# A transposed accumulator: the accumulator of a streaming cross-attention is kept in blocks of 32x32, VectorE transposes in place of TensorE, and the probabilities are transposed one head at a time

## The chip, the cores and the metric

The kernel runs on one core of a Trainium2 chip. The metric is the device time of one execution in microseconds.

## The reference

A set of 512 queries (M, 512x512) attends over 6250 inputs x (6250x256) with 8 heads of 64; then follow an output projection, a layer norm, a feed-forward block of width 2048 and a second layer norm. Everything is float32.

```python
q = (M @ Wq.T).reshape(e, h, dh).transpose(1, 0, 2)
kv = x @ Wkv.T + bkv
k, v = jnp.split(kv, 2, axis=-1)
...
sim = jnp.einsum('hid,hjd->hij', q, k) * dh ** (-0.5)
sim = jnp.where(mask, sim, -1000000000.0)
attn = jax.nn.softmax(sim, axis=-1)
out = jnp.einsum('hij,hjd->hid', attn, v)
out = out.transpose(1, 0, 2).reshape(e, h * dh)
out = out @ Wo.T + bo
m = layer_norm(out + M)
ffn = jax.nn.relu(m @ W1.T + b1) @ W2.T + b2
z = layer_norm(ffn + m)
```

## The kernel before

**Tiling.** The keys are padded to 7 chunks of 896. The 8 heads are 4 pairs; two heads of 64 fill the 128 partitions. The 512 queries are 4 tiles of 128. A chunk holds 4 pairs, and a pair 4 tiles, so there are 28 pairs and 112 tiles. Products other than the one with V are made from a high and a low part of each operand (three matmuls in place of one).

**One tile (S, E, X).** TensorE writes the scores of a query tile, both heads, into two of three PSUM slots of 1024 columns (line 889). VectorE adds the mask (`lower`), takes the running minimum of the negated scores and writes them to `prob` (line 734, one instruction for each head). ScalarE takes the exponential in place and sums the rows (line 579, one for each head). VectorE then transposes both heads' 1792 columns in blocks of 32x32 from `prob` into `st` (line 744, step X). In the order of the steps X of a tile stands behind the two minima of the next tile, and the first of these minima waits for the X before it (`prob` has two buffers).

**The moves (M, B).** Blocks of 32x32 are transposed in place, so the quarters of partitions have to change places: 16 DMAs for each half pair (two tiles) carry `st` into `pt`, twelve issued by SyncE (M, line 387), four by ScalarE (B, line 631). X of the first tile of a half waits until the moves of the pair before have landed.

**The values (W, C, F, A).** Two pairs later TensorE multiplies `val` with `pt` over 7 key tiles (W, line 943; fp32, four passes each), which gives outT with head dimensions on partitions and 512 queries in columns. ScalarE copies it to SBUF (C, line 610), TensorE transposes it with four matmuls against the identity (F, line 952), and VectorE adds it to the accumulator `acc`, queries on partitions (A, line 751).

**The rest of a pair.** K makes the next pair's keys (line 815), ScalarE copies them (H, line 602) and GpSimd splits them (L). V makes a value tile of the next chunk, copied by ScalarE (line 588). Z updates the statistics: GpSimd takes the difference of maxima (`drop`), ScalarE its exponential (`alpha`, line 635), and GpSimd scales the row sums and `acc` (line 472), one factor for each query and head. J and R load and split x, Q loads the mask.

**The end.** After the last pair N divides `acc` by the row sums (line 757), G transposes it on TensorE (line 963), T and D add the bias and split it (lines 614 and 760), and Y projects with Wo (line 847), for pairs 0 and 1, then 2, then 3. The two last pairs' W, C, F and A lie between these.

**What sets the order.** It is written out by hand. `ROUNDS` (line 52) has a string for each tile of each pair, `FIRST` (line 74) those of the first two pairs, and `chunk_schedule` (line 86) turns them into one list of steps, with a list of its own for the end. Each engine walks the same list and takes its own steps in that order, so a step's place in the list is its place in each queue. Semaphores tie the engines together.

```python
for c in range(CHUNKS):
    body(c, chunk_schedule(c == 0, c == CHUNKS - 1), c % 2)
```

## Time and profile before

| | |
|---|---|
| median of three runs | 683.79 us (680.31, 683.79, 1226.24) |
| the profiled execution | 684.72 us, span 682.9 us |
| TensorE matmul | 632.4 us busy (93%), 3382 instructions |
| VectorE | 549.7 us busy (80%), 685 instructions |
| ScalarE | 363.8 us busy (53%), 659 instructions |
| GpSimd | 254.8 us busy (37%), 312 instructions |
| attention (first scores to last exponential) | 20 to 541 us |
| output projection, norms, feed-forward | from there to the end |
| granted TensorE clock | 0.98 of full speed, mean |

The page gives one profiled execution. The span is the time from its first to its last instruction. Engines work side by side, so their busy times do not add up to it. A matmul's end is modelled, and a matmul overlaps the next, so TensorE is read better by the starts of its instructions. A line of a timeline has the start, the duration, the engine, the line of the program, what is written from what, and in brackets how long the engine had been idle before and who released it. DMA issues are shown on the queue of the engine that issues them (SPq, ACTq).

### The profile page before, as it was taken

The page shows a single profiled execution, that of the slowest core. Times are in us where ns is not written, and L with a number is a line of the kernel's source. Part 1 is how long each engine was busy: PE and PEld are TensorE (multiplying, and loading weights), DVE is VectorE, ACT ScalarE, POOL GpSimd, SP SyncE. Part 2 cuts the span into 40 slices and gives each one's busy share as a digit, 9 for nine tenths or more (in the row PEclk, how much of TensorE's full clock was granted, in tenths as well). Part 3 has the DMA queues.
Part 4 walks back from the last instruction along what each step waited for, and adds up shares of the span by engine and source line. Part 5 has one row for each costly group of instructions (what it writes and reads, how often), then busy time and mean ns, then how long its engine had stood idle before and what let it go on. Part 6 is the DMA issues. An engine that isn't in the chain of part 4 may idle for free.

```text
span 682.9 us, 10600 instructions
## 1 busy us (share of the span) xinstructions
PE 632.4 (93%) x3382; PEld 396.0 (58%) x3382; DVE 549.7 (80%) x685; ACT 363.8 (53%) x659; POOL 254.8 (37%) x312
## 2 busy tenths in 40 slices
PE   4999999999999999999999999999998697999996
PEld 3675555545665555655555566555653344688884
DVE  3889999999998999899999999899998836334334
ACT  5576565565565566556565565556564313333332
POOL 3561632264224632163226522363212404422224
PEclk9999999999999999999999999999999898799999
DMA  8078989878988889888997888888777982032221
GB/s 285 9 201 210 221 215 254 206 201 211 230 222 206 216 215 252 192 206 209 233 230 196 212 223 227 204 218 207 198 194 187 257 231 72 31 93 93 92 91 61
DMA packets 56098, 128.29 MB, mean 188 GB/s; under 512 B 15856, under 2 KB 20976, under 8 KB 55792
## 3 DMA queue, kind: packets, MB, share of 16 engines
q1 hardware_dynamic: 45296, 101.97, 58.2%
q10 hardware_dynamic: 10752, 25.70, 14.1%
q8 instruction: 25, 0.41, 0.3%
q14 instruction: 25, 0.20, 0.1%
HBM read 23.80 MB, written 1.05 MB: 36 GB/s over the span
## 4 chain that ended last, share of the span: by engine, by line
PE 59%; DVE 16%; issue 7%; SPq 5%; ACT 4%; POOL 3%; DMA 3%; ACTq 2%; DVEq 0%; POOLq 0%
PE tail L943 16%; PE slot L889 13%; DVE st L744 7%; PE tail L815 7%; PE slot L1001 7%; PE slot L996 7%; PE slot L815 6%; SPq L387 4%; DVE prob L734 4%; ACT prob L579 2%; PE tail L952 2%; ACTq L631 2%; DVE acc L751 2%; DMA wq_raw<-in_wq 1%; PE slot L847 1%
## 5 line engine op out<-in xcount | busy, mean ns | idle before, releaser
L579 ACT ACTIVATE prob<-prob,negmax 128x896 f32<-128x896 f32 x224 | 233.6, 1043 | 203.9 <-DVE negmax L734 201.4
L734 DVE CUSTOM_DVE_ANT_0 prob<-slot,lower,negmax_old 128x896 f32<-128x896 f32 x224 | 248.9, 1149 | 36.1 <-PE slot L889 25.4
L744 DVE STREAM_TRANSPOSE st<-prob 128x1792 f32<-128x1792 f32 x112 | 228.5, 2040 | 4.9 <-DMA pt<-st 4.7
L943 PE MATMUL tail<-pt,val 128*64 128x512 f32 x784 | 184.5, 607 | 8.1 <-ACT outT_sb L610 5.9
L943 PEld LDWEIGHTS tail<-pt,val 128*64 128x64 f32 x784 | 51.4, 138 | 102.9 <-issue 94.4
L889 PE MATMUL slot<-k_hi,q_hi 64*128 64x448 f32 x448 | 94.8, 414 | 10.9 <-DVE negmax L734 6.8
L889 PEld LDWEIGHTS slot<-k_hi,q_hi 64*128 64x128 f32 x448 | 43.3, 183 | 78.7 <-issue 71.2
L889 PE MATMUL slot<-k_hi,q_lo 64*128 64x448 f32 x448 | 84.0, 363 | 0.0
L889 PE MATMUL slot<-k_lo,q_hi 64*128 64x448 f32 x448 | 83.7, 362 | 0.0
L467 POOL TENSOR_TENSOR total<-total,alpha 128x8 f32<-128x8 f32 x28 | 5.8, 206 | 189.6 <-ACT alpha L635 189.5
L489 POOL TENSOR_TENSOR k_lo<-k_raw,k_hi 128x896 fp32r<-128x896 f32 x27 | 57.1, 2115 | 3.9 <-POOL k_hi L486 0.2
L442 POOL TENSOR_SCALAR lower<-mask_raw 128x896 bf16<-128x896 uint8 x28 | 27.1, 968 | 52.8 <-DVE negmax L734 41.8
L889 PEld LDWEIGHTS slot<-k_hi,q_lo 64*128 64x128 f32 x448 | 43.8, 184 | 2.6
L889 PEld LDWEIGHTS slot<-k_lo,q_hi 64*128 64x128 f32 x448 | 43.8, 185 | 1.1
L524 POOL TENSOR_TENSOR hid_lo<-hid,hid_hi 128x512 fp32r<-128x512 f32 x15 | 20.6, 1371 | 62.2 <-DVE hid_hi L799 62.2
L815 PE MATMUL tail<-wv_hi,x_hi 128*128 128x512 f32 x98 | 35.7, 445 | 6.9 <-ACT val L588 6.8
L579 ACT ACTIVATION_READ_ACCUMULATOR prob<-prob,negmax 128x1 f32 x224 | 41.7, 186 | 0.0
L815 PE MATMUL slot<-x_hi,wk_hi 128*128 128x448 f32 x112 | 33.5, 381 | 8.3 <-ACT x_hi L554 8.3
L799 DVE CAST hid_hi<-hid 128x512 fp32r<-128x512 f32 x15 | 6.4, 428 | 33.9 <-ACT hid L670 33.8
L815 PE MATMUL slot<-x_lo,wk_hi 128*128 128x448 f32 x112 | 32.6, 373 | 0.0
L815 PE MATMUL slot<-x_hi,wk_lo 128*128 128x448 f32 x112 | 32.3, 370 | 0.0
L670 ACT ACTIVATE hid<-slot,b_sb 128x512 f32<-128x512 f32 x16 | 11.0, 690 | 36.8 <-PE slot L996 36.8
(127 smaller groups left out, 844.6 us busy)
## 6 DMA issues: line engine op xcount, KB each, us to landing
pt<-st SPq DMA_DIRECT2D x672, 112.0 KB, 3.0
pt<-st ACTq DMA_DIRECT2D x224, 112.0 KB, 3.4
w_raw<-in_w SPq DMA_DIRECT2D x32, 256.0 KB, 2.9
x_raw<-in_x SPq DMA_DIRECT2D x13, 448.0 KB, 4.3
mask_raw<-in_mask SPq DMA_DIRECT2D x7, 448.0 KB, 4.5
mt_raw<-in_mt SPq DMA_DIRECT2D x2, 512.0 KB, 7.8
wo_raw<-in_wo SPq DMA_DIRECT2D x1, 1024.0 KB, 6.9
m_res<-in_mn SPq DMA_DIRECT2D x1, 1024.0 KB, 5.1
```

The costliest lines, as they stand in the source:

```text
L387: sp.dma_start(pt[LANES * b:LANES * b + LANES, buf, a], st[LANES * a:LANES * a + LANES, i, b]).then_inc(landed[buf], 16)
L442: nc.gpsimd.tensor_scalar(lower[:, t], mask_raw[:, t], -1.0, -BIG, ALU.add, ALU.mult).then_inc(lower_ready, 1)
L489: nc.gpsimd.tensor_tensor(kst[1][:, p % 2], k_raw[:], kst[0][:, p % 2], ALU.subtract).then_inc(klo_done, 1)
L524: nc.gpsimd.tensor_tensor(hid_split(i + j, j, 1), hid[:, j], hid_split(i + j, j, 0), ALU.subtract).then_inc(hidlo, 1)
L579: nc.scalar.activation(unit, unit, ACT.Exp, bias=negmax[:, p, u:u + 1], scale=-1.0, accum_out=psumrow[:, p, u:u + 1]).then_inc(exp_done, 1)
L734: nc.vector.tensor_tensor_reduce(out=prob[:, i % 2, h].rearrange("p (b n) -> p b n", b=2), in0=slot[:, j, :, :HALF], in1=lower[:, i].rearr ...
L744: nc.vector.transpose(st[:, g].rearrange("p b k (t i) -> p k b t i", t=2)[:, :, :, t2], prob[:, i % 2].rearrange("p h (k b i) -> p (h k) b ...
L815: last = nc.tensor.matmul(dst, stationary(a, k), moving(b, k), start=(n == 0), stop=(n == len(terms) - 1))
L889: last = nc.tensor.matmul(slot[:, j, b, :HALF], q2[qa][rows(h), p, P * i:P * i + P], key_half(p, b, kb)[rows(h)], start=(part == 0), stop= ...
L943: last = nc.tensor.matmul(outT[DH * h:DH * h + DH], val[:, val_at(i, parity ^ (p < 0)), head(p, h)], moving, start=(i == 0), stop=(i == KT ...
L996: last = nc.tensor.matmul(slot[:, 2, j], w12[a][:, j, k], mT2[b][:, k], start=(i == 0), stop=(i == len(terms) - 1))
L1001: last = nc.tensor.matmul(slot[:, t // 2, t % 2], hid_split(n, j, a)[:, P * t:P * t + P], w2_split(n, j, b), start=first and i == 0, stop= ...
```

## The change

The accumulator is kept as VectorE's block transpose leaves it: partition 32 d + i holds query i of a block of 32 and block d of the 128 head dimensions; the columns are 16 query blocks of 32 dimensions.

- C is a VectorE transpose of outT from PSUM into SBUF, in the place of ScalarE's copy; it moves from the third tile of a pair to the fourth, between the minima and X. F, the four TensorE transposes, is gone.
- A, the add, is done by GpSimd in all pairs but the last two of the last chunk, from SBUF.
- The factor `alpha` is needed for each query block and head in the new layout: 16 small ScalarE exponentials of 32 partitions by 4 columns (step e, eight in the third and eight in the fourth tile) write it from `drop` into `alpha_blk`. The scaling of `acc` by GpSimd becomes a step of its own (z) in the first tile of the next pair, three tiles later than before.
- X is two transposes of 896 columns, one for each head, each with its own count of `xposed`; each minimum waits only for its own head's half.
- At the end the reciprocal of the row sums is spread with 16 copies a pair (step i), G is a VectorE transpose into `prob`, and T and D read it from there. Y of pairs 0 and 1 stands wholly between the value products of the last two pairs, where it used to start before them.

```diff
-    ('S E0 E1 W0 W1 W2 W3 X M1 R0',
+    ('S E0 E1 W0 W1 W2 W3 X M1 R0 z',
      'S E0 V1 E1 Z K H L X B1',
-     'S E0 E1 F W4 W5 W6 C A X M0 Q',
-     'S E0 E1 V2 X B0'),
-    ('S E0 E1 W0 W1 W2 W3 X M1',
+     'S E0 E1 W4 W5 W6 X e0 M0 Q',
+     'S E0 E1 V2 C A X e1 B0'),
+    ('S E0 E1 W0 W1 W2 W3 X M1 z',
      'S E0 V3 E1 Z K H L X B1',
-     'S E0 E1 F W4 W5 W6 C A X M0',
-     'S E0 E1 V4 X B0'),
-    ('S E0 V5 E1 W0 W1 X M1',
+     'S E0 E1 W4 W5 W6 X e0 M0',
+     'S E0 E1 V4 C A X e1 B0'),
+    ('S E0 V5 E1 W0 W1 X M1 z',
      'S E0 V6 E1 Z K H J0 L X B1',
-     'S E0 E1 F W2 W3 W4 A X R1 M0',
-     'S E0 E1 W5 W6 C X B0 J1 I'),
-    ('S E0 E1 W0 W1 W2 W3 X M1',
-     'S E0 E1 Z F K H L A X B1',
-     'S E0 E1 W4 W5 W6 C X M0',
-     'S E0 E1 N0 X B0 O'),
+     'S E0 E1 W2 W3 W4 X e0 R1 M0',
+     'S E0 E1 W5 W6 C A X e1 B0 J1 I'),
+    ('S E0 E1 W0 W1 W2 W3 X M1 z',
+     'S E0 E1 Z K H L X B1',
+     'S E0 E1 W4 W5 W6 X e0 M0',
+     'S E0 E1 N0 C A X e1 B0 O'),
...
-                elif kind in "WC":
+                elif kind in "WCA":
                     step = (kind, p - 2, i)
-                elif kind in "FA":
-                    step = (kind, p - 3, i)
                 elif kind in "KHL":
                     step = (kind, p + 1, i)
                 elif kind in "MB":
                     step = (kind, p - i, i)
-                elif kind == "Z":
+                elif kind in "Ze":
                     step = (kind, p - 1, i)
+                elif kind == "z":
+                    step = (kind, p - 2, i)
                 if first and step[1] < 0 or last and (kind in "JRQ" or step[1] == PAIRS) or not last and kind in "IO":
                     continue
                 out.append(step)
-                if kind == "A" and last and step[1] >= 0:
-                    out.append(("N", step[1], 0))
     if last:
         a, b = PAIRS - 2, PAIRS - 1
-        out.extend([("F", 1, 0), ("A", 1, 0), ("N", 1, 0)])
-        out.extend([("X", b, 3), ("M", b, 1), ("B", b, 1), ("Z", b, 0), ("I", b, 1), ("O", b, 1)])
-        out.extend([("G", 0, 0), ("T", 0, 0), ("D", 0, 0)])
-        out.extend([*(("W", a, kt) for kt in range(3)), ("G", 1, 0), ("T", 1, 0), ("D", 1, 0)])
-        out.extend([*(("W", a, kt) for kt in range(3, KT)), ("C", a, 0), ("Y", 0, 0), ("F", a, 0), ("A", a, 0), ("N", a, 0)])
-        out.extend([("Y", 0, 1), ("Y", 0, 2), ("Y", 0, 3), ("G", a, 0), ("T", a, 0), ("D", a, 0)])
-        out.extend([*(("W", b, kt) for kt in range(KT)), ("C", b, 0), ("Y", 1, 0), ("F", b, 0), ("A", b, 0), ("N", b, 0)])
-        out.extend([("Y", 1, 1), ("Y", 1, 2), ("Y", 1, 3), ("G", b, 0), ("T", b, 0), ("D", b, 0)])
-        out.extend([("Y", 2, t) for t in range(QT)])
+        out.extend([("X", b, 3), ("M", b, 1), ("B", b, 1), ("Z", b, 0), ("e", b, 0), ("e", b, 1), ("z", a, 0), ("z", b, 0)])
+        out.extend([("I", b, 1), ("O", b, 1), ("i", 0, 0), ("N", 0, 0), ("G", 0, 0), ("i", 1, 0), ("N", 1, 0), ("G", 1, 0)])
+        out.extend([("T", 0, 0), ("D", 0, 0), ("T", 1, 0), ("D", 1, 0), ("i", a, 0)])
+        out.extend([*(("W", a, kt) for kt in range(KT)), ("C", a, 0), ("A", a, 0), ("N", a, 0), ("G", a, 0), ("T", a, 0), ("D", a, 0)])
+        out.extend([*(("Y", 0, t) for t in range(QT)), ("i", b, 0)])
+        out.extend([*(("W", b, kt) for kt in range(KT)), ("C", b, 0), ("A", b, 0), ("N", b, 0), ("G", b, 0), ("T", b, 0), ("D", b, 0)])
+        out.extend([*(("Y", 1, t) for t in range(QT)), *(("Y", 2, t) for t in range(QT))])
...
+        def per_block(stat, p):
+            return stat[:, p].unsqueeze(2).to_broadcast([P, BLOCKS, LANES])
+
+        def quadrants(*heads):
+
+            for dims in (d for h in heads for d in (2 * h, 2 * h + 1)):
+                for queries in range(QUAD):
+                    yield dims, queries, dims // 2
+
+        def block_stat(stat, p, dims, queries):
+
+            own = stat[LANES * dims:LANES * dims + LANES, p]
+            return own.rearrange("p (g q t) -> p q g t", g=2, q=QUAD)[:, queries]
+
+        def tile_stat(stat, p, queries, h):
+            own = stat[LANES * queries:LANES * queries + LANES, p, QT * h:QT * h + QT]
+            return own.rearrange("p (g t) -> p g t", g=2)
+
+        def by_block(t):
+            return t.rearrange("p (b i) -> p b i", b=BLOCKS)
+
+        def ao_raw(p):
+            return prob[:, p // 2, p % 2, :E]
...
+                    if kind == "z":
+                        n, own = pair_no(c, p), p % PAIRS
+                        blocks = in_register(pool, QUAD * QUAD * (n + 1))
                         if is_past(n, PAIRS):
                             pool.wait_ge(acc_added, n - PAIRS + 1)
-                        nc.gpsimd.tensor_tensor(by_head(acc[:, own]), by_head(acc[:, own]), per_head(alpha, own), ALU.mult).then_inc(acc_scaled, 1)
+                        pool.wait_ge(zeroed, 2)
+                        pool.wait_ge(alpha_blk_ready, blocks)
+                        nc.gpsimd.tensor_tensor(acc[:, own], acc[:, own], per_block(alpha_blk, own), ALU.mult).then_inc(acc_scaled, 1)
...
+                    if kind == "A" and not (final and p >= PAIRS - 2):
+                        posed, own = in_register(pool, pair_no(c, p) + 1), acc[:, p % PAIRS]
+                        pool.wait_ge(zeroed, 2)
+                        pool.wait_ge(acc_scaled, posed)
+                        pool.wait_ge(outT_copied, posed)
+                        nc.gpsimd.tensor_tensor(own, own, by_block(outT_sb[:]), ALU.add).then_inc(acc_added, 1)
...
-                    if kind == "C":
-                        act.wait_ge(pv_done, KT * (n + 1))
-                        if isinstance(n, int) and n == 0:
-                            act.wait_ge(qlo_done, PAIRS)
-                        if is_past(n, 1):
-                            act.wait_ge(f_filled, n)
-                        nc.scalar.copy(outT_sb[:].rearrange("p (g t a i) -> p g a t i", g=2, a=QUAD, t=2),
-                                       outT.rearrange("p (g a t i) -> p g a t i", g=2, a=QUAD, t=2)).then_inc(outT_copied, 1)
                     if kind == "T":
-                        act.wait_ge(aoT_filled, p + 1)
-                        nc.scalar.activation(ao2[0][:, p], gather_bank(p), ACT.Identity, bias=bv_sb[:, p:p + 1]).then_inc(aohi, 1)
+                        act.wait_ge(ao_ready, p + 1)
+                        nc.scalar.activation(ao2[0][:, p], ao_raw(p), ACT.Identity, bias=bv_sb[:, p:p + 1]).then_inc(aohi, 1)
...
+                    if kind == "e":
+                        if is_past(n, PAIRS):
+                            act.wait_ge(acc_scaled, n - PAIRS + 1)
+                        for dims, queries, h in quadrants(i):
+                            nc.scalar.activation(block_stat(alpha_blk, p % PAIRS, dims, queries), tile_stat(drop, p % PAIRS, queries, h),
+                                                 ACT.Exp).then_inc(alpha_blk_ready, 1)
...
-                        free = in_register(dve, QT * n + i - 1) if is_past(QT * n + i, 2) else None
                         for h in range(2):
                             j, before = unit_use(c, p, i, h)
                             written, u = in_register(dve, before + 1), QT * h + i
+                            free = in_register(dve, 2 * (QT * n + i - 2) + h + 1) if is_past(QT * n + i, 2) else None
                             dve.wait_ge(zeroed, 2)
-                            if h == 0 and free is not None:
+                            if free is not None:
...
-                        dve.wait_ge(exp_done, U * n + 2 * i + 2)
-                        nc.vector.transpose(
-                            st[:, g].rearrange("p b k (t i) -> p k b t i", t=2)[:, :, :, t2],
-                            prob[:, i % 2].rearrange("p h (k b i) -> p (h k) b i", b=QUAD, i=LANES)).then_inc(xposed, 1)
-                    if kind == "A":
+                        for h in range(2):
+                            dve.wait_ge(exp_done, U * n + 2 * i + h + 1)
+                            nc.vector.transpose(
+                                st[:, g].rearrange("p b (h k) (t i) -> p h k b t i", h=2, t=2)[:, h, :, :, t2],
+                                prob[:, i % 2, h].rearrange("p (k b i) -> p k b i", b=QUAD, i=LANES)).then_inc(xposed, 1)
+                    if kind == "C":
+                        read, done = in_register(dve, n) if is_past(n, 1) else None, in_register(dve, KT * (n + 1))
+                        dve.wait_ge(zeroed, 2)
+                        if read is not None:
+                            dve.wait_ge(acc_added, read)
+                        if isinstance(n, int) and n == 0:
+                            dve.wait_ge(qlo_done, PAIRS)
+                        dve.wait_ge(pv_done, done)
+                        nc.vector.transpose(by_block(outT_sb[:]), by_block(outT)).then_inc(outT_copied, 1)
+                    if kind == "A" and final and p >= PAIRS - 2:
                         dve.wait_ge(acc_scaled, n + 1)
-                        dve.wait_ge(f_filled, n + 1)
-                        own = acc[:, p % PAIRS].rearrange("p t n -> p (t n)")
-                        nc.vector.tensor_tensor(own, own, tp, ALU.add).then_inc(acc_added, 1)
-                    if kind == "N":
+                        dve.wait_ge(outT_copied, n + 1)
+                        nc.vector.tensor_tensor(acc[:, p], acc[:, p], by_block(outT_sb[:]), ALU.add).then_inc(acc_added, 1)
+                    if kind == "i":
                         dve.wait_ge(stats_kept, 2 * (n + 1))
                         nc.vector.reciprocal(inv[:, p], total[:, p]).then_inc(inv_ready, 1)
+                        dve.wait_ge(inv_ready, p + 1)
+                        dve.wait_ge(acc_scaled, n + 1)
+                        for dims, queries, h in quadrants(0, 1):
+                            nc.vector.tensor_copy(block_stat(alpha_blk, p, dims, queries), tile_stat(inv, p, queries, h)).then_inc(inv_blk_ready, 1)
+                    if kind == "N":
+                        dve.wait_ge(inv_blk_ready, QUAD * QUAD * (p + 1))
                         dve.wait_ge(acc_added, n + 1)
-                        dve.wait_ge(inv_ready, p + 1)
-                        nc.vector.tensor_tensor(by_head(acc[:, p]), by_head(acc[:, p]), per_head(inv, p), ALU.mult).then_inc(norm_ready, 1)
+                        nc.vector.tensor_tensor(acc[:, p], acc[:, p], per_block(alpha_blk, p), ALU.mult).then_inc(norm_ready, 1)
+                    if kind == "G":
+                        dve.wait_ge(norm_ready, p + 1)
+                        dve.wait_ge(xposed, QT * PAIRS * CHUNKS)
+                        nc.vector.transpose(ao_raw(p).rearrange("p (g t q i) -> p g q t i", g=2, t=2, q=QUAD),
+                                            acc[:, p].rearrange("p (g q t) i -> p g q t i", g=2, q=QUAD)).then_inc(ao_ready, 1)
...
-                    if kind == "F":
-                        if isinstance(n, int) and n == 0:
-                            pe.wait_ge(ident_ready, 1)
-                        tp_free(c, banks[step])
-                        pe.wait_ge(outT_copied, n + 1)
-                        for t in range(QT):
-                            last = nc.tensor.transpose(tp[:, P * t:P * t + P], outT_sb[:, P * t:P * t + P], ident[:])
-                        last.then_inc(f_filled, 1)
-                    if kind == "G":
-                        pe.wait_ge(norm_ready, p + 1)
-                        if p == 0:
+                    if kind == "Y":
+                        if p == 0 and i == 0:
                             emptied = dict(unit_use(c, PAIRS - 1, t, h) for t in range(QT) for h in range(2))
                             for j in range(RING):
                                 pe.wait_ge(drained[j], emptied[j] + 1)
-                        if p >= 2:
-                            pe.wait_ge(aolo, p - 1)
-                        for t in range(QT):
-                            last = nc.tensor.transpose(gather_bank(p)[:, P * t:P * t + P], acc[:, p, t], ident[:])
-                        last.then_inc(aoT_filled, 1)
```

## Rows read from the trace of the kernel before

**Rows 1.** Busy time by stretch, chunk 2; columns: stretch, us, engines (instructions), clock, DMA, GB/s.

```profile
169.28:243.80 74.52, 71.75 (x414) 42.34 (x410) 69.42 (x85) 44.42 (x84) 28.97 (x36) 1.00 0.87 218
```

**Rows 2.** Groups by line: line, engine, operation, shapes, count, busy us, mean ns, idle before.

```profile
L734 DVE CUSTOM_DVE_ANT_0 prob<-slot,lower,negmax_old 128x896 f32<-128x896 f32 x224 | 248.9, 1149 | 36.1 <-PE slot L889 25.4 <-DVE st L744 0.5
...
L538 POOL TENSOR_TENSOR m_res<-norm,b_sb 128x512 f32<-128x512 f32 x4 | 5.0, 1276 | 0.0
...
L757 DVE TENSOR_TENSOR acc<-acc,inv 128x512 f32<-128x512 f32 x4 | 2.8, 692 | 0.4
...
L708 DVE TENSOR_TENSOR wq_lo<-wq_raw,wq_hi 128x1536 fp32r<-128x1536 f32 x1 | 1.7, 1749 | 0.0
```

**Rows 3.** Timeline of VectorE, 326 to 342: start us, us, engine, line, operation, idle before.

```profile
326.18 1.15 DVE L734 CUSTOM_DVE_ANT_0 prob<-slot,lower,negmax_old 128x896 f32<-128x896 f32 x1 [0.60 <-PE slot L889]
...
328.33 0.69 DVE L751 TENSOR_TENSOR acc<-acc,tail 128x512 f32<-128x512 f32 x1
328.93 2.04 DVE L744 STREAM_TRANSPOSE st<-prob 128x1792 f32<-128x1792 f32 x1
331.10 1.15 DVE L734 CUSTOM_DVE_ANT_0 prob<-slot,lower,negmax_old 128x896 f32<-128x896 f32 x1
...
342.00 2.04 DVE L744 STREAM_TRANSPOSE st<-prob 128x1792 f32<-128x1792 f32 x1
```

**Rows 4.** Timeline of TensorE, 320 to 330: one pair's steps by their starts.

```profile
320.50 0.74 PE L815 MATMUL tail<-wv_hi,x_hi 128*128 128x512 f32 x2
...
322.00 0.57 PE L815 MATMUL slot<-x_hi,wk_hi 128*128 128x448 f32 x2
...
324.53 0.48 PE L889 MATMUL slot<-k_hi,q_hi 64*128 64x448 f32 x2
...
325.94 0.66 PE L952 MATMUL tail<-ident,outT_sb 128*128 128x128 f32 x4
326.52 2.79 PE L943 MATMUL tail<-pt,val 128*64 128x512 f32 x12
329.25 0.47 PE L889 MATMUL slot<-k_hi,q_hi 64*128 64x448 f32 x2
```

**Rows 5.** Timeline of all engines, 498 to 503: the V copy that TensorE waits for.

```profile
498.67 1.15 DVE L734 CUSTOM_DVE_ANT_0 prob<-slot,lower,negmax_old 128x896 f32<-128x896 f32 x1
...
501.98 0.56 ACT L588 COPY val<-tail 128x512 f32<-128x512 f32 x1
...
502.60 0.73 PE L815 MATMUL tail<-wv_hi,x_hi 128*128 128x512 f32 x2 [1.12 <-ACT val L588]
```

**Rows 6.** Timeline of ScalarE, 325 us: small exponential, K copy, issue of moves.

```profile
325.13 0.20 ACT L635 ACTIVATE alpha<-drop 128x8 f32<-128x8 f32 x1
325.23 1.00 ACT L602 ACTIVATE k_raw<-slot,bk_sb 128x896 f32<-128x896 f32 x1
325.26 2.45 ACTq L631 DMA_DIRECT2D pt<-st  x3
```

**Rows 7.** Timeline of VectorE, from 542: operations that follow without a wait.

```profile
542.46 2.05 DVE L744 STREAM_TRANSPOSE st<-prob 128x1792 f32<-128x1792 f32 x1 [2.86 <-DMA pt<-st]
544.43 0.65 DVE L751 TENSOR_TENSOR acc<-acc,tail 128x512 f32<-128x512 f32 x1
...
574.79 0.18 DVE L770 BATCH_NORM_AGGREGATE meanvar<-stats 128x2 f32<-128x6 f32 x1
574.89 0.66 DVE L766 TENSOR_TENSOR norm<-slot,m_res 128x512 f32<-128x512 f32 x1
```

**Rows 8.** Timeline of SyncE, 331 us: the twelve moves of two tiles.

```profile
331.07 7.89 SPq L387 DMA_DIRECT2D pt<-st  x12
```

**Rows 9.** The chain of waits that ended last, from 553: start us, us, engine, line.

```profile
553.16 1.63 PE slot L847 x6
...
559.77 6.16 PE tail L943 x28
...
571.62 1.20 DVE w_lo L774 x2
```

38 lines of the change are left out of this document (13 added, 25 removed), and 5 rows, old and new, of the table FIRST.

## The prediction

> **What bounds the kernel now.** First the busy times by stretch: a whole chunk takes 74.5 us [rows 1], so a pair costs 18.6 and the 28 pairs three quarters of the span. In it VectorE is busy 69.4 us, TensorE 71.8; ScalarE 44, GpSimd 29. Two engines near 95% need the timeline. VectorE's own work per query tile is two masked minima and one block transpose. From the start of the first minimum to the accumulator add is 2.15 us, and the transpose takes 2.17 from its start to the next minimum (328.93 to 331.10) although its row says 2.04 [rows 3]: that minimum waits for the transpose right before it on its own engine. The add takes 0.60. A chunk of VectorE's work is thus 16 x 4.32 + 4 x 0.60 = 71.5 us, and the other 3.0 of the 74.5 are waits for scores, as at 326.18; the group of minima counts 25.4 us of them in all [rows 2]. TensorE is read by its starts, since ends are modelled [rows 4]: scores of a tile 1.41 us, a V tile 1.50, K 2.53, the four transposes 0.58, three value products 2.73 (0.91 each). A chunk of that is 16 x 1.41 + 7 x 1.50 + 4 x 2.53 + 4 x 0.58 + 28 x 0.91 = 71.0 us. So **VectorE (71.5) and TensorE (71.0) bound it together**, and 3.0 us are lost because each is late for the other at times.
>
> **Price of half a transpose.** A tensor_tensor takes 692 ns at 512 columns and 1749 at 1536 [rows 2]: 1.03 ns a column. The 1792 columns of the transpose are then 1.85 us of its 2.04, with 0.19 fixed; a half is 0.92 + 0.19 = 1.11 long. The only transpose that is followed by something that does not wait for it starts at 542.46 and lasts 2.05, and its successor starts at 544.43, 0.08 before its end [rows 7]; so an unheld half occupies 1.03. In the new order the next tile's first minimum needs only the first half, which by then has long ended, so nothing is held: 2.07 a tile against 2.17. Bounds: 0.98 a half (a pipelined fixed part of 0.06, as the add at 328.33 shows with 0.60 for 512 columns) and 1.24 (its length and the held gap of 0.13 as well). I take 1.035, since the transpose's own row is the nearest.
> The Trainium skill speaks against this part ("VectorE: DVE Perf Modes", The DRAIN you can't avoid): no VectorE operation starts until the one before has emptied the pipe, the semaphore costs nothing, so the number of operations is what to keep low. The trace agrees only in part: the held transpose costs 0.13 more than its length and the unheld one 0.08 less [rows 3, 7]. By the rows the sum is 669; by that rule a half costs up to its length and a gap, and the sum is the slow rival's.
>
> **VectorE, the rest.** It loses the add (0.60, four a chunk) and gets the copy of outT as a block transpose of 512 columns: 0.53 + 0.19 - 0.08 = 0.64; from PSUM no dearer, as the add read PSUM too. Bounds 0.53 and 0.85. The add goes to GpSimd: 1.28 us by its two-operand row of 512 columns [rows 2], 5.1 a chunk on an engine at 29 of 74; behind it there queue the split of x (third pair) and the scaling, wanted a tile later. Nothing, while GpSimd stays two tiles ahead. VectorE then has 16 x 4.22 + 4 x 0.64 = 70.1 us a chunk.
>
> **TensorE** loses the transposes, 2.3 us: 68.7 a chunk.
>
> **Both together**, a pair from the start of its predecessor's last tile (0). The first value product now waits for the new outT transpose, which stands behind two minima: 2.15 + 0.71 + 0.1 = 2.96. Then 4 x 0.91 to 6.60, scores, V, K (1.41 + 1.50 + 2.53) to 12.04, the next scores; VectorE gets them 1.65 later (324.53 to 326.18 [rows 3, 4]) at 13.69, but was free at 0.64 + 3 x 4.22 = 13.30: a wait of 0.39. The last tile starts 4.22 later, 17.91. This holds for the first two pairs of a chunk. In the third a V product comes first, and it waits for ScalarE's copy of the V before, which ends 3.87 after the last tile's start and let TensorE idle 1.12 [rows 5]; that copy stands ahead of the new exponentials, so this stays: 3.93 + 1.50 + 1.82 + 1.41 + 1.50 + 2.53 = 12.69, VectorE at 14.34, the last tile at 18.56. The fourth has no V there and VectorE alone sets 0.64 + 4 x 4.22 = 17.52. Chunk: 17.91 x 2 + 18.56 + 17.52 = **71.9 us, 2.6 less**. Five such chunks give 13.0; the last one, to its final pair, 1.8; the first, which has neither add nor transposes in its first pairs, about 1.3. Together 16.1.
>
> **ScalarE** loses the copy (0.57 a pair) and gets 16 exponentials of 32x4. A small one lasts 0.20, but its successor starts 0.10 after it [rows 6]: 1.6 us a pair, at most 3.2. Eight stand between the V copy and the issue of four moves, at 3.87 to 4.7 (5.5). That issue blocks the queue, 0.6 each (SyncE: 7.89 for twelve) to 0.8 (ScalarE: three in 2.45 [rows 6, 8]): to 7.2 (8.8), and the next tile's exponentials start there instead of at 0.64 + 4.22 + 1.2 = 6.1. Their own transpose does not feel it: it comes at 0.64 + 2 x 4.22 + 2.15 = 11.2, and they end at 9.5 (11.1). In the third pair a V copy stands behind the first of them, wanted by TensorE at 8.7 and there at 8.9 (10.5): 0.2 to 1.8 a chunk. I take the low end and count nothing, since the small exponential's spacing and SyncE's issue are the cleaner rows; the high end is 11 us in all.
>
> **Moves.** SyncE needs 7.89 us for its twelve, started when the second tile is transposed; the transpose that reuses the buffer started at 342.00, 11.03 after the one at 328.93 ended [rows 3, 8]. In the new order VectorE comes there after 0.64 + 2 x 4.22 + 2.15 = 11.2. Hidden by 0.2 us; without it each tenth counts.
>
> **The end.** Its clock starts at 542.46, where a transpose waits for a landed move; the 1 MB load of Wo ahead sets that, not the changed work. Now (from there): output projection at 10.7, last value products at 17.3, last ao_lo done at 29.2 [rows 7, 9]. New: two transposes to 4.2 (before, add, reciprocal and product stood between them); then for pairs 0 and 1 reciprocal and sixteen copies of 32x4 at 0.10 each (574.79 to 574.89 [rows 7]; at most 0.20), product, transpose: 1.9 + 0.8 + 0.8, twice, to 11.2; two ao_lo, 12.6. The projection comes at 12.6, its 24 products now all ahead of the last value products: 5.5 (559.77 less 553.16, less two sets of transposes) to 18.1; value products 6.2 to 24.3; then transpose, add, product, transpose, ao_hi, ao_lo in a chain, some 0.8 each, instead of copy, PE transposes, add, product, PE transposes and the same two: 29.3. **0.1 slower**, between 1 faster and 4 slower.
>
> **Sum.** The profiled execution took 684.72 (span 682.9), 0.9 above the median of 683.79. -16.1 + 0.1 = -16.0: **669 us**.
>
> **Rivals.**
> *More than that*: the waits between the two engines vanish, and a chunk falls to VectorE's 70.1: 4.4 x 6.2 = 27, 657 us. For it, TensorE has 3.2 us less work than its time; against it, the wait on V's copy is untouched. 0.12, between 657 and 663.
> *Moves or ScalarE become the bound.* The reuse at 11.2 has 0.2 of cover. Landings 0.5 slower than at 342.00 (3.1 after the last issue) take it and 0.3 more, 0.3 x 28 = 9 us back, 678; small exponentials of 0.20 and issues of 0.8 give 11 us, 680. For it, the DMA engines are already at 0.87 [rows 1], and a shorter chunk makes that 0.90; against it, hardly a transpose waits for a landing now. 0.23.
> *Slower: back-to-back transposes hold each other.* Place: the pair of halves in each tile. Each costs its length and the held gap, 1.24, so a tile takes 2.15 + 2.48 = 4.63 and a chunk 16 x 4.63 + 2.6 = 76.7: 2.2 more, 14 in all, **699 us**. It decides from 1.17 a half. For it speaks that no row shows a transpose behind a transpose, against it 544.43 [rows 7]. The skill's rule named above is this case. 0.13.
> That the change does not do what it says: the transposes and the add leave these engines by the order itself; no chance of its own.
>
> **Numbers.** Forecast 0.52, from 663 to 675, two thirds of it below 670. A difference under 2% (13.7 us) is what a measurement of this kernel can't tell from none. Faster: 0.34 + 0.12 = 0.46; within: 0.18 + 0.23 = 0.41; slower 0.13. The range 660 to 685 leaves out the slow rival and the lower half of the first, together just under 0.2.
>
> **What would show it.** Starts of consecutive half transposes 1.03 apart, the next minimum right behind (1.24: the slow rival). Chunk stretches of 71.9. Waits for scores down from 25.4 to about 11 us, one of 1.05 in each third pair. Waits of half transposes for moves: none long. Small exponentials 0.10 apart. Projection 12.6 after the landed move at the end. Wrong would make it a transpose from PSUM dearer than 0.85, or GpSimd so late with the scaling that the adds and splits behind it hold K.

## The result, and the profile after

The changed kernel takes 687.96 us in the median of 11 runs (685.43 to 691.68), against 684.03 for the kernel before on the same chip: a ratio of 1.0068 [1.0051, 1.0085], 0.7% slower. The forecast was 669 us, between 660 and 685. (Its sum starts from the profiled execution of the kernel before; from the median it gives 668.) The profiled execution took 689.07 us, its span is 686.9 (before 684.72 and 682.9).

Three moments of the profile and its span divide the loss. The first moment is the start of the transpose in the last pair that waits for a landed move, where the forecast's clock for the end starts.

| kernel | that transpose | projection starts | first layer norm | span |
|---|---|---|---|---|
| before | 542.46 | 553.16 | 573.34 | 682.9 |
| after | 540.09 | 557.42 | 578.46 | 686.9 |

So the attention part became 2.4 us shorter where 16.1 were forecast, the end to the first norm went from 30.9 to 38.4 where 31.0 was forecast, and the rest became 1.1 shorter. (-2.4 + 7.5 - 1.1 = +4.0, the difference of the spans.)

The stretch of chunk 2 in the changed kernel answers to [rows 1]:

```profile
168.32:242.16 73.84, 69.76 (x398) 40.70 (x396) 69.14 (x102) 55.00 (x144) 34.27 (x40) 1.00 0.87 216
```

TensorE is 2.0 us less busy, as it should be without the transposes, ScalarE 10.6 more, and the chunk only 0.68 shorter. Over the first six chunks the mean is 74.4 us in both kernels. The groups by line, which answer to [rows 2], show where VectorE's time is:

```profile
L755 DVE CUSTOM_DVE_ANT_0 prob<-slot,lower,negmax_old 128x896 f32<-128x896 f32 x224 | 245.8, 1133 | 16.9 <-PE slot L927 16.4 <-DVE st L766 0.2
L766 DVE STREAM_TRANSPOSE st<-prob 128x896 f32<-128x896 f32 x224 | 234.3, 1084 | 24.2 <-DMA pt<-st 24.2
...
L655 ACT ACTIVATE alpha_blk<-drop 32x4 f32<-32x4 f32 x448 | 90.8, 203 | 10.2
...
L504 POOL TENSOR_TENSOR acc<-acc,outT_sb 128x512 f32<-128x512 f32 x26 | 33.3, 1280 | 75.5 <-DVE outT_sb L777 75.0
...
L788 DVE COPY alpha_blk<-inv 32x4 f32<-32x4 f32 x64 | 12.6, 196 | 2.0
```

Waits for scores fell from 25.4 to 16.4 us, but the half transposes now wait 24.2 us for moves, in 24 places. In the kernel before (line, what was waited for, us in total, times, longest):

```profile
DVE st L744 <- DMA pt<-st: 4.7, 6, 2.9
```

VectorE's own operations are as cheap as hoped. Its timeline in pair 12 (to be read like [rows 3]):

```profile
253.59 2.10 DVE L766 STREAM_TRANSPOSE st<-prob 128x896 f32<-128x896 f32 x2
255.61 1.11 DVE L755 CUSTOM_DVE_ANT_0 prob<-slot,lower,negmax_old 128x896 f32<-128x896 f32 x1
256.65 1.14 DVE L755 CUSTOM_DVE_ANT_0 prob<-slot,lower,negmax_old 128x896 f32<-128x896 f32 x1
257.72 0.71 DVE L777 STREAM_TRANSPOSE outT_sb<-tail 128x512 f32<-128x512 f32 x1
258.36 2.06 DVE L766 STREAM_TRANSPOSE st<-prob 128x896 f32<-128x896 f32 x2
...
268.69 2.10 DVE L766 STREAM_TRANSPOSE st<-prob 128x896 f32<-128x896 f32 x2 [2.02 <-DMA pt<-st]
```

Two halves take 2.02 from the first start to the next minimum (253.59 to 255.61), 1.01 each, and the transpose of outT occupies 0.64 (257.72 to 258.36). The tile is 4.13 us. The last line is the new wait. The moves that it waits for, on ScalarE (also [rows 6]) and on SyncE (also [rows 8]):

```profile
258.88 0.56 ACT L611 COPY val<-tail 128x512 f32<-128x512 f32 x1
259.47 0.89 ACT L655 ACTIVATE alpha_blk<-drop 32x4 f32<-32x4 f32 x4
260.24 0.52 ACTq L646 DMA_DIRECT2D pt<-st  x1
...
261.68 1.27 ACTq L646 DMA_DIRECT2D pt<-st  x2
263.00 1.04 ACT L602 ACTIVATE prob<-prob,negmax 128x896 f32<-128x896 f32 x1 [1.74 <-issue]
```

```profile
255.77 7.52 SPq L399 DMA_DIRECT2D pt<-st  x12
```

The tile was transposed at 255.69. SyncE issues its twelve at once, ScalarE its four between 260.24 and 262.95, 4.55 us later; in the kernel before it was 2.84 in the same pair (256.50 to this line):

```profile
259.34 0.51 ACTq L631 DMA_DIRECT2D pt<-st  x1
```

How busy the DMA engines were meanwhile, in four stretches (the columns of [rows 1]):

```profile
255.70:260.20 4.50, 4.06 (x24) 2.14 (x24) 4.50 (x7) 4.10 (x13) 1.28 (x1) 1.00 0.81 241
260.20:263.00 2.80, 2.80 (x20) 1.30 (x18) 2.80 (x6) 0.97 (x6) 1.41 (x3) 1.00 0.89 209
263.00:266.00 3.00, 3.00 (x17) 2.35 (x14) 3.00 (x5) 2.54 (x5) 0.00 (x0) 1.00 1.05 254
266.00:268.70 2.70, 2.70 (x20) 2.17 (x18) 0.68 (x3) 2.70 (x7) 0.21 (x1) 1.00 1.03 282
```

The DMA share is 0.81 and 0.89 until ScalarE's four are issued, then full to the landing. In the kernel before the same four stretches have 0.90, 0.94, 1.03 and 0.98. The chain of waits says the same of the last of SyncE's moves, which lands 5.97 us after its issue began and 5.4 after it ended (263.29); in the forecast's rows the latter was 3.0 [rows 3, 8]:

```profile
262.70 5.97 DMA pt<-st
```

Pair 12 has the longest wait of this kind before the last pair. The landings in the traces, taken over pairs 6 to 23 for the moves of a pair's first two tiles, give these means:

| mean, us | before | after |
|---|---|---|
| second tile transposed, to ScalarE's first issue | 2.6 | 4.5 |
| second tile transposed, to the last of the sixteen landings | 10.8 | 11.7 |
| end of SyncE's last issue, to that landing | 2.3 | 3.1 |

Of the 24.2 us of waits 20.0 are for these moves, before 1.6. The moves of a pair's other two tiles have no small exponentials right ahead of their issue, and there the waits are about as before (4.2 and 3.2, most of it in the last pair).

At the end, the timelines of VectorE, TensorE and GpSimd:

```profile
540.09 4.09 DVE L766 STREAM_TRANSPOSE st<-prob 128x896 f32<-128x896 f32 x4 [3.00 <-DMA pt<-st]
...
544.30 4.50 DVE L788 COPY alpha_blk<-inv 32x4 f32<-32x4 f32 x16
...
550.39 3.87 DVE L788 COPY alpha_blk<-inv 32x4 f32<-32x4 f32 x16
...
557.42 3.04 DVE L788 COPY alpha_blk<-inv 32x4 f32<-32x4 f32 x16
...
561.32 4.52 DVE L781 TENSOR_TENSOR acc<-acc,outT_sb 128x512 f32<-128x512 f32 x1
```

```profile
557.42 0.76 PE L887 MATMUL slot<-wo_hi,ao_hi 128*128 128x512 f32 x1 [8.68 <-DVE ao_lo L800]
557.98 0.63 PE L887 MATMUL slot<-wo_lo,ao_hi 128*128 128x512 f32 x1
558.41 0.63 PE L887 MATMUL slot<-wo_hi,ao_lo 128*128 128x512 f32 x1
...
562.59 0.40 PE L887 MATMUL slot<-wo_lo,ao_hi 128*128 128x512 f32 x1
562.82 0.39 PE L887 MATMUL slot<-wo_hi,ao_lo 128*128 128x512 f32 x1
```

```profile
540.44 4.53 POOL L537 TENSOR_TENSOR wo_lo<-wo_raw,wo_hi 128x2048 fp32r<-128x2048 f32 x1
...
560.70 4.58 POOL L541 TENSOR_TENSOR m_res<-m_res,bo_sb 128x2048 f32<-128x2048 f32 x1 [8.97 <-DMA b_sb<-in_b]
```

Sixteen copies take 3.04 us undisturbed, 0.19 each, and more in the first two pairs. The projection starts 17.3 us after the landed move instead of 12.6, and TensorE, idle for 8.68 us, begins its 24 products 0.43 apart and goes over to 0.23 only at 562.1. And an add of 512 columns that takes 0.69 elsewhere takes 4.52; it ends at 565.84, 0.56 after GpSimd's long add has ended (565.28).

### The profile page after: what moved, and what is told of

It is laid out like the page before. It is cut to its first block, busy times and chain, and to the rows that moved or that the text cites. A ratio compares the mean times of both kernels' runs of the same rounds, so it can differ in the third digit from the quotient of the medians.

```text
span 686.9 us, 10979 instructions
## 1 busy us (share of the span) xinstructions
PE 620.1 (90%) x3254; PEld 385.0 (56%) x3254; DVE 568.1 (83%) x867; ACT 438.3 (64%) x1079; POOL 288.8 (42%) x338
## 3 DMA queue, kind: packets, MB, share of 16 engines
HBM read 23.80 MB, written 1.05 MB: 36 GB/s over the span
## 4 chain that ended last, share of the span: by engine, by line
PE 32%; SPq 22%; DVE 21%; DMA 9%; issue 7%; ACT 5%; ACTq 2%; POOL 0%; DVEq 0%; POOLq 0%
SPq L399 22%; DVE st L766 10%; DMA pt<-st 8%; PE slot L1020 7%; PE slot L1025 7%; PE tail L981 6%; PE slot L927 5%; DVE prob L755 5%; PE tail L855 3%; PE slot L855 3%; ACT prob L602 3%; DVE alpha_blk L788 2%; PE tail L940 2%; ACTq L646 1%; DMA wq_raw<-in_wq 1%
## 5 line engine op out<-in xcount | busy, mean ns | idle before, releaser
L755 DVE CUSTOM_DVE_ANT_0 prob<-slot,lower,negmax_old 128x896 f32<-128x896 f32 x224 | 245.8, 1133 | 16.9 <-PE slot L927 16.4
L766 DVE STREAM_TRANSPOSE st<-prob 128x896 f32<-128x896 f32 x224 | 234.3, 1084 | 24.2 <-DMA pt<-st 24.2
L655 ACT ACTIVATE alpha_blk<-drop 32x4 f32<-32x4 f32 x448 | 90.8, 203 | 10.2
L504 POOL TENSOR_TENSOR acc<-acc,outT_sb 128x512 f32<-128x512 f32 x26 | 33.3, 1280 | 75.5 <-DVE outT_sb L777 75.0
L855 PE MATMUL tail<-wv_hi,x_hi 128*128 128x512 f32 x98 | 36.5, 455 | 10.3 <-ACT val L611 10.3
L489 POOL TENSOR_TENSOR acc<-acc,alpha_blk 128x512 f32<-128x512 f32 x28 | 29.4, 1051 | 37.9 <-ACT alpha_blk L655 37.4
```

The lines of the kernel that those rows point to most:

```text
L504: nc.gpsimd.tensor_tensor(own, own, by_block(outT_sb[:]), ALU.add).then_inc(acc_added, 1)
L655: nc.scalar.activation(block_stat(alpha_blk, p % PAIRS, dims, queries), tile_stat(drop, p % PAIRS, queries, h), ACT.Exp).then_inc(alpha_bl ...
L755: nc.vector.tensor_tensor_reduce(out=prob[:, i % 2, h].rearrange("p (b n) -> p b n", b=2), in0=slot[:, j, :, :HALF], in1=lower[:, i].rearr ...
L766: nc.vector.transpose(st[:, g].rearrange("p b (h k) (t i) -> p h k b t i", h=2, t=2)[:, h, :, :, t2], prob[:, i % 2, h].rearrange("p (k b ...
L855: last = nc.tensor.matmul(dst, stationary(a, k), moving(b, k), start=(n == 0), stop=(n == len(terms) - 1))
```

## Experiments

**e1: the four moves of ScalarE before the small exponentials** (in all six strings that have them).

```diff
-     'S E0 E1 V2 C A X e1 B0'),
+     'S E0 E1 V2 C A X B0 e1'),
```

> The eight small exponentials of the fourth tile stand behind the issue of ScalarE's four moves instead of ahead of it. Theory A (ScalarE's late issue is what makes the first transposes of a pair wait for landings): the issue starts 2.5 us after the transpose again instead of 4.5, the waits of half transposes for moves fall from 24.2 us to under 8, chunks from 74.4 to about 72.5, the time by 8 to 13 us to 675 to 680. Theory B (the moves of SyncE, 7.9 us of issue and 3.1 to land, bound the faster VectorE whatever ScalarE does): waits for moves stay above 15 us and the time moves by less than 3 us. Theory C (the exponentials hurt by holding the next tile's exponentials and V copy): the same delay of these, only later, so the waits for scores stay or grow, and the time stays within 3 us.

Measured: 679.50 us, ratio 0.9936 [0.9916, 0.9956], 8.5 us under the changed kernel. Queues of ScalarE and SyncE and VectorE's waiting transpose in the same pair:

```profile
254.95 1.16 ACTq L646 DMA_DIRECT2D pt<-st  x2
...
256.14 1.71 ACTq L646 DMA_DIRECT2D pt<-st  x2
257.89 1.80 ACT L655 ACTIVATE alpha_blk<-drop 32x4 f32<-32x4 f32 x8 [1.50 <-issue]
```

```profile
252.73 8.01 SPq L399 DMA_DIRECT2D pt<-st  x12
```

```profile
264.05 2.10 DVE L766 STREAM_TRANSPOSE st<-prob 128x896 f32<-128x896 f32 x2 [0.43 <-DMA pt<-st]
```

```profile
252.70:255.00 2.30, 2.30 (x18) 1.71 (x16) 2.30 (x5) 1.98 (x7) 0.00 (x0) 1.00 0.77 161
255.00:258.00 3.00, 2.92 (x16) 0.92 (x14) 3.00 (x4) 1.50 (x4) 1.28 (x1) 1.00 1.03 305
258.00:261.00 3.00, 3.00 (x21) 1.69 (x18) 3.00 (x6) 2.81 (x11) 1.15 (x2) 1.00 1.05 265
```

ScalarE's four start 2.2 us after SyncE's first, the DMA share is full from there, and the landing is 11.3 us after SyncE's first issue instead of 12.9. Over the whole run the waits for moves fall from 24.2 to 15.0 us, the chunks to a mean of 72.7, and the last pair's landed move comes at 529.78. The means of the table above are 2.3, 11.0 and 2.2 here. The place of these four moves is thus worth 10.3 of the 13.7 us that the attention part fell short, in these two profiles; the end is 1.0 longer than in the changed kernel (39.4) and the rest 0.8. The time agrees with theory A and is against B and C. But A expected waits for moves under 8 us, and the 15.0 left are at B's bound: the late issue made about half of their rise from 4.7 to 24.2.

**e2: one exponential in the place of a pair's sixteen.**

```diff
-                        for dims, queries, h in quadrants(i):
-                            nc.scalar.activation(block_stat(alpha_blk, p % PAIRS, dims, queries), tile_stat(drop, p % PAIRS, queries, h),
-                                                 ACT.Exp).then_inc(alpha_blk_ready, 1)
+                        if i == 0:
+                            nc.scalar.activation(alpha_blk[:, p % PAIRS].rearrange("p (a b) -> p a b", b=2),
+                                                 drop[:, p % PAIRS].unsqueeze(2).to_broadcast([P, U, 2]), ACT.Exp).then_inc(alpha_blk_ready, 1)
```

> The sixteen small exponentials of a pair are one of 128x16, so the factors are not spread as the layout needs (that part of the computation is left out). All else is the changed kernel. Theory A: ScalarE gets back 3.4 us a pair, moves are issued in time, chunks of about 72.0 (the forecast's 71.9), 14 to 17 us less than the changed kernel, about 672. Theory B: under 4 us less. Theory C: as A, but the waits for scores fall as well, from 16.4 us to about 11.

Measured: 678.76 us, 0.9926 [0.9900, 0.9952]; waits for moves 13.8 us. No better than e1, which keeps all sixteen: it is the issue behind them that costs, not ScalarE's time for them. Theory A expected 672 and waits nearly gone, and missed by 7 us: with no small exponentials at all, and moves issued as early as in e1, more than half of the waits for moves stay.

**e3: the transpose of the probabilities in one piece again**, 1792 columns, the rest as changed.

```diff
-                        for h in range(2):
-                            dve.wait_ge(exp_done, U * n + 2 * i + h + 1)
-                            nc.vector.transpose(...
+                        dve.wait_ge(exp_done, U * n + 2 * i + 2)
+                        nc.vector.transpose(
+                            st[:, g].rearrange("p b k (t i) -> p k b t i", t=2)[:, :, :, t2],
+                            prob[:, i % 2].rearrange("p h (k b i) -> p (h k) b i", b=QUAD, i=LANES)).then_inc(xposed, 2)
```

> The changed kernel with both heads transposed by one instruction again. If the split is what gave VectorE 4.13 a tile, the tile is 4.32 again: 16 x 0.19 = 3.0 us a chunk where VectorE is the bound. Theory A and B: where the moves bind anyway (one wait a pair) a part of it is hidden; 5 to 12 us slower than the changed kernel, 693 to 700. If the split were worth nothing, 688.

Measured: 694.48 us, 1.0135 [1.0103, 1.0167], 6.5 us above the changed kernel. The held gap is back:

```profile
257.03 2.04 DVE L765 STREAM_TRANSPOSE st<-prob 128x1792 f32<-128x1792 f32 x1
259.20 1.15 DVE L755 CUSTOM_DVE_ANT_0 prob<-slot,lower,negmax_old 128x896 f32<-128x896 f32 x1
```

2.17 to the next minimum, against 2.02 for two halves.

**e4: the kernel before with the split transpose alone** (the reverse of e3's edit in the kernel before, the counts that SyncE and ScalarE wait for doubled).

> The kernel before with the split alone: two transposes of 896 and the minima waiting for their own head's half. VectorE has 4.13 a tile with no small exponentials ahead of the moves. Theory A: a chunk falls from 74.5 by up to 3, less what TensorE (71.0 with its transposes) and the moves take back; 672 to 678. Theory B: the moves bind here as well, waits for moves rise from 4.7 to over 15 us, and the time is 681 to 685.

Measured: 676.82 us, 0.9894 [0.9872, 0.9916]. The split is worth 7.3 us by itself, and the end, unchanged, keeps its 30.9 (535.07 to 565.96). The changed kernel is 11.1 us slower than this one. In the attention part that is the order of the new steps and not the layout: with the moves issued first (e1) the last pair's landed move comes at 529.78, 5.3 earlier than here. What e1 loses to this kernel it loses at the end (39.4 against 30.9).

**e5: one copy in the place of a pair's sixteen at the end.**

```diff
-                        for dims, queries, h in quadrants(0, 1):
-                            nc.vector.tensor_copy(block_stat(alpha_blk, p, dims, queries), tile_stat(inv, p, queries, h)).then_inc(inv_blk_ready, 1)
+                        nc.vector.tensor_copy(alpha_blk[:, p].rearrange("p (a b) -> p a b", b=2),
+                                              inv[:, p].unsqueeze(2).to_broadcast([P, U, 2])).then_inc(inv_blk_ready, 1)
```

> The changed kernel, with the sixteen copies that spread each pair's reciprocals at the end done as one of 128x16, so the last factors are not spread as the layout needs (left out). Theory A says that the end lost 7.6 us because a run of such copies takes 0.19 to 0.28 each instead of 0.10: 32 of them stand ahead of the projection. Without them the projection starts when ScalarE is through with its own small exponentials, some 11 to 12 us after the landed move instead of 17.3, and the value products behind it 6 us earlier: 6 to 8 us less than the changed kernel, 680 to 682. A rival: the end is set by the granted clock and by the landing of the last moves, and the time falls by under 2.

Measured: 680.83 us, 0.9954 [0.9935, 0.9973], 7.1 under the changed kernel. Its profile has a span 8.7 shorter. Of that, 4.3 is the end (34.1 from 534.95 to 569.04); but the attention part is 5.1 shorter too, although nothing in it differs, mostly in chunks 3 to 5. Why was not settled. The executions of the changed kernel themselves spread over 6 us, and there is one profile for each kernel, so a division of a profile's loss between attention and end is sure to a few microseconds only, that of e1 included. The runs of e1 (at most 680.57) and of the changed kernel (at least 685.43) don't overlap. The median lies where it was expected (680 to 682) partly by luck: the projection starts 13.8 us after the landed move instead of the expected 11 to 12, and the attention part made up for it. A single copy of 16 columns, seen on VectorE and on GpSimd:

```profile
539.16 3.12 DVE L787 COPY alpha_blk<-inv 128x16 f32<-128x16 f32 x1
```

```profile
537.73 4.51 POOL L537 TENSOR_TENSOR wo_lo<-wo_raw,wo_hi 128x2048 fp32r<-128x2048 f32 x1
```

It takes 3.12 us and ends at 542.28, where GpSimd's subtraction ends (542.24); the same copy at 548.73 takes 0.17.

**e6: the spreading of pairs 0 and 1 moved ahead, into the waits of the last pair**, on top of e1.

```diff
+                if last and p == PAIRS - 1 and kind == "X" and t in (1, 3):
+                    out.extend([("i", 0, 0)] if t == 1 else [("N", 0, 0), ("i", 1, 0)])
                 out.append(step)
```

> The small exponentials behind ScalarE's moves as in e1, and the spreading of pairs 0 and 1 put where VectorE waits for moves in the last pair (before its first and third transposes). Nothing is left out. Theory A: most of the 8 us of copies lie in waits; against e1 (679.5) 4 to 6 us less, 673.5 to 675.5. If VectorE's waits there are not free (the transposes they delay are themselves awaited), the gain is under 2.

Measured: 683.82 us, 1.0019 [0.9995, 1.0042], 4.3 slower than e1: a miss. The copies of pair 1 have met GpSimd's work on Wo:

```profile
530.54 9.73 DVE L790 COPY alpha_blk<-inv 32x4 f32<-32x4 f32 x16
...
560.44 4.45 DVE L802 SCALAR_TENSOR_TENSOR ao_lo<-prob,bv_sb,ao_hi 128x512 fp32r<-128x512 f32 x1 [0.79 <-ACT ao_hi L631]
```

```profile
529.99 1.52 POOL L506 TENSOR_TENSOR acc<-acc,outT_sb 128x512 f32<-128x512 f32 x1 [10.56 <-DVE outT_sb L779]
531.46 1.88 POOL L537 CAST wo_hi<-wo_raw 128x2048 fp32r<-128x2048 f32 x1
533.43 4.50 POOL L539 TENSOR_TENSOR wo_lo<-wo_raw,wo_hi 128x2048 fp32r<-128x2048 f32 x1
...
559.78 4.56 POOL L543 TENSOR_TENSOR m_res<-m_res,bo_sb 128x2048 f32<-128x2048 f32 x1 [7.61 <-DMA b_sb<-in_b]
```

They take 9.73 us instead of 3.04. One of them, started at 533.59 right behind the start of GpSimd's subtraction, lasts 4.37 to 537.96, when that is done (537.93); the twelve behind it stand 0.19 apart again.

**e7: as e6, but the second eight exponentials of a pair in the next pair's first tile**, away from the moves altogether.

> As e6, but the second eight small exponentials stand in the first tile of the next pair, where ScalarE has no moves to issue, instead of behind the fourth tile's moves. Theory A: the same or up to 3 us better than e6, since neither moves nor the next exponentials wait for them; GpSimd's scaling comes 4 us later, which nobody waits for.

Measured: 688.06 us, 1.0059 [1.0027, 1.0090], 4.2 slower than e6: a miss. Of the 4.4 us between the profiles, 2.8 is the end (36.9 against 34.1): ao_hi of pairs 0 and 1 stands behind eight more small exponentials in ScalarE's queue, and VectorE waits 7.23 us for it instead of 5.21. The last chunk starts 1.5 later as well (458.74 and 457.29). The moves of all pairs being free of the small exponentials brought nothing beyond e6.

**e8: as e6, the bias's add to the residual by GpSimd only after pair 2's add.**

```diff
                         pool.wait_ge(bias_in, 16 * 4)
+                        pool.wait_ge(acc_added, PAIRS * CHUNKS - 1)
```

> As e6, but GpSimd's addition of bo to the residual (4.6 us) waits until VectorE has added pair 2's products. In the changed kernel that VectorE add of 128x512 took 4.52 us while GpSimd's ran. If the two held each other, the add takes 0.7 here, and the time falls by the 0.6 us for which the last outT transpose was late, at most 1; the GpSimd addition must still be done before the first layer norm, 12 us later. If the add was long for another reason, it stays near 4.5.

Measured: 684.06 us, 1.0002 [0.9981, 1.0023], as e6. The add took 0.69, but the next operation that reads two SBUF operands, ao_lo's, met the moved instruction and took 4.20: the hold had only changed its victim.

**e9: as e6, GpSimd's work on Wo only after the thirty-two copies.**

```diff
                         pool.wait_ge(wo_in, 16)
+                        pool.wait_ge(inv_blk_ready, 2 * QUAD * QUAD)
```

> As e6, but GpSimd splits Wo only when VectorE has spread the reciprocals of pairs 0 and 1. In e6 sixteen copies of 32x4 took 9.73 us while GpSimd split Wo (1.88 and 4.50 us), in a quiet stretch 3.04. If a VectorE copy from SBUF to SBUF and a GpSimd instruction hold each other, the sixteen take 3.0 to 3.3 here and the transposes behind them come 6.5 us earlier: against e6 (683.8) 4 to 7 us less, 677 to 680. If the copies were slow for another reason (the landing moves in SBUF, ScalarE), they stay above 8 us and the time at 683 to 685.

Measured: 678.62 us, 0.9921 [0.9901, 0.9940], 5.2 less than e6. The copies of pair 1 take 3.89 (the first of them still under GpSimd's add), and GpSimd starts behind them:

```profile
528.93 3.89 DVE L791 COPY alpha_blk<-inv 32x4 f32<-32x4 f32 x16
```

```profile
532.96 1.89 POOL L538 CAST wo_hi<-wo_raw 128x2048 fp32r<-128x2048 f32 x1 [3.03 <-DVE alpha_blk L791]
```

9.73 less 3.89 is 5.8 us, about the whole difference. That the copies and GpSimd's work hold each other is thus shown by order alone.

**e10: the reciprocals spread by ScalarE**, on top of e1: sixteen activations a pair in place of VectorE's copies, for pairs 0 and 1 in the last pair's second and fourth tiles; the last pair's exponentials go behind T and D of pairs 0 and 1, and the product N of pair 0 goes ahead of the last tile's transpose.

```diff
-                            nc.vector.tensor_copy(block_stat(alpha_blk, p, dims, queries), tile_stat(inv, p, queries, h)).then_inc(inv_blk_ready, 1)
...
+                    if kind == "i":
+                        act.wait_ge(inv_ready, p + 1)
+                        act.wait_ge(acc_scaled, n + 1)
+                        for dims, queries, h in quadrants(0, 1):
+                            nc.scalar.activation(block_stat(alpha_blk, p, dims, queries), tile_stat(inv, p, queries, h),
+                                                 ACT.Identity).then_inc(inv_blk_ready, 1)
```

> As e1 (small exponentials behind the moves), and at the end ScalarE instead of VectorE spreads the reciprocals, for pairs 0 and 1 in the last pair's second and fourth tiles, with the small exponentials of the last pair behind the projection's operands of pairs 0 and 1. Nothing is left out. ScalarE has ports of its own, so GpSimd's split of Wo should not hold the spreading: sixteen in 3.6 us whatever GpSimd does. Projection 6 us earlier than in e1 (there 17.8 after the landed move), 673 to 676 in all. If ScalarE's queue becomes the chain at the end (moves of the last tiles 2 to 4 us later), 677 to 681.

Measured: 673.99 us, 0.9857 [0.9834, 0.9879]; faster than both kernels, by 10 and 14 us. The projection starts at 544.41, 14.5 us after the landed move (17.9 in e1, of which 6 were expected to go). What remains on VectorE is a product that met GpSimd's subtraction:

```profile
532.01 4.42 DVE L796 TENSOR_TENSOR acc<-acc,alpha_blk 128x512 f32<-128x512 f32 x1
```

**e11 and e12: GpSimd's two instructions of 4.5 us cut into four of 512 columns**, in e10 and in e6.

```diff
-                        nc.gpsimd.tensor_tensor(wo2[1][:], wo_raw[:], wo2[0][:], ALU.subtract).then_inc(wolo, 1)
+                        for k in range(4):
+                            nc.gpsimd.tensor_tensor(wo2[1][:, k], wo_raw[:, k], wo2[0][:, k], ALU.subtract).then_inc(wolo, 1)
```

> The spreading by ScalarE as in e10, and GpSimd's two long instructions at the end, the low part of Wo and the residual's bias (4.5 us each), cut into four of 512 columns. If VectorE's operations between SBUF and SBUF stand still for the whole of the GpSimd instruction that they meet, then the first product of the end (4.42 us in e10, 0.69 undisturbed) can be held by no more than one piece, so it takes under 2.0, the ao_lo that took 3.29 under 2.0, and the median falls by 1 to 4 us below e10's 674.0: 670 to 673. If the two only share bandwidth for as long as both have work, cutting changes nothing: the product takes 4 again, 674.

> e6 with the same cut. Here sixteen copies of 32x4 by VectorE met the GpSimd work on Wo and took 9.73 us. If a piece is held to its own end and VectorE gets a turn between two pieces for one copy, the copies still take about as long as GpSimd's work lasts, 8 to 10 us, and the median stays at 683.8, less what the later product gains (0 to 3 us): 681 to 684. If VectorE keeps its turn once it has it, the copies take about 5 and the median is about 679, as in e9.

Measured: e11 672.85 us, 0.9842 [0.9799, 0.9886], the fastest of all, though not told apart from e10 in time; e12 685.37 us, 1.0019 [0.9991, 1.0047], as e6. In e11 the product and, on GpSimd, the pieces:

```profile
535.20 1.44 DVE L798 TENSOR_TENSOR acc<-acc,alpha_blk 128x512 f32<-128x512 f32 x1
```

```profile
533.59 5.41 POOL L540 TENSOR_TENSOR wo_lo<-wo_raw,wo_hi 128x512 fp32r<-128x512 f32 x4
```

1.44 instead of 4.42, and ao_lo's 3.29 became 1.01: one operation is held for what is left of one piece. In e12 the sixteen copies still take 9.61, as the first theory had it: one copy is held for 1.1 to 1.2 us at each of the four pieces, and cutting doesn't help them.

## Why the prediction was wrong, point by point

- **Half transposes: right, and a little cheap.** 1.01 for the 1.035 forecast; the tile is 4.13 (forecast 4.22), because the minimum behind an unheld transpose is shorter as well (1.11). The slow rival (1.24 a half) is refuted by the spacing, by e3 and by e4, which puts the split at 7 us. The Trainium skill's rule that was weighed there ("VectorE: DVE Perf Modes", The DRAIN you can't avoid) would have made the split a loss, read as the prediction read it; the measurement decides against that reading. The section adds that an operation which is not held starts earlier; the forecast's rows and 1.01 agree with that.
- **outT's transpose, the add on GpSimd, TensorE without transposes: right.** 0.64 (forecast 0.64), 1.28 (1.28), and 2.0 us a chunk less on TensorE (2.3). VectorE has 16 x 4.13 + 4 x 0.64 = 68.6 us of work a chunk. The other 5.8 of the 74.4 are waits: 24.2 for moves and 16.4 for scores, over seven chunks.
- **The step that failed: "Moves ... Hidden by 0.2 us".** It followed SyncE's twelve to their landing and took 3 us for that from the old order. ScalarE's four, whose issue the step before had put at 7.2 us after the last tile's start (measured 7.34: 255.61 to 262.95), were priced only for what they do to the next exponentials. But all sixteen share the DMA engines, which are nearly full [rows 1]; while the four are held back the engines are partly idle, and SyncE's last moves then land later. From the transpose to the last landing it was 13.0 us in pair 12 (255.69 to 268.67), 10.9 before; on average 11.7, 10.8 before. VectorE was back after 11.0 (forecast 11.2), so a cover of 0.2 became a wait of 0.7 on average and of 2.0 in pair 12. This is the rival "Moves or ScalarE become the bound", given 0.23; it priced landings 0.5 slower without saying why they should be, and that alone as 9 us. e1 confirms it by order alone, and the other traces agree: in the three kernels where ScalarE's first issue comes 4.5 to 4.7 us after the transpose (changed, e3, e5) the last landing follows SyncE's last issue by 3.1 to 3.2 us on average, in all the others, with 2.3 to 2.6, by 2.2 to 2.4. What e1 does not give back, 3.4 of the 13.7 us, is probably waits for moves too (15.0 us in all), as the cover of 0.2 leaves no room for landings that vary by a microsecond and more; no run separates that. Most of it is lost early: chunks 3 and 4 of e1 take 72.0, as forecast (71.9), chunks 0 to 2 a mean of 73.2.
- **Spacing of small operations.** In a row, the exponentials stand 0.22 apart (eight in 1.79, line 655) and the copies 0.19, not 0.10. In both rows that gave 0.10 [rows 6, 7] the successor was another kind of operation, with PSUM as a source; no row had two of the small ones in succession. The bound of 0.20 was named (0.22 is above even that), and the low value taken. For the exponentials it cost little: the first of ScalarE's moves was issued at 260.24, 4.63 us after the last tile's start (forecast 4.7), before the last four of the eight had run. For the copies it was 1.4 us a pair. The Trainium skill ("VectorE: DVE Perf Modes", The TRN2 errata) says that operations with an SBUF source pay a fixed extra latency for each instruction, and to avoid many small tiles; the 0.19 for four columns agrees.
- **The end: 0.1 slower forecast, 7.5 measured.** The copies of the first two pairs took 8.4 instead of 3.2 (2.9 by their spacing, 2.3 held by GpSimd), so the projection came 4.7 late. Its 24 products took 7.8 instead of 5.5, by the clock: over 555 to 560 the granted clock was 0.50 after 8.68 us of an idle TensorE, and the first ten products stood 0.43 apart against 0.23. That is the lower of the two levels, 1.2 GHz. Then an add was held for 3.8 us more than its 0.69; of that only some 0.7 reached the end, since the transpose behind this work (572.14) needs the last value products, done at 571.43. 4.7, 2.3 and 0.7 account for the 7.5. The term's upper bound, 4, was too low, as the contention had no place in it.
- **The third pair's wait for V**: one of 1.05 forecast, two of 1.55 and 1.18 in pair 14. Of small weight.
